# Three row buffers, weights loaded on another condition, Y cleared from SyncE's queue, and redrawn places, in a Mamba layer with routed experts

## What is computed

```python
h = x + mamba(layernorm(x), ...)              # scan: h_t = exp(dt*A) * h_(t-1) + dt*x * B_t, 16 states, 512 channels
m = gelu(layernorm(h) @ mlp_w1.T + mlp_b1) @ mlp_w2.T + mlp_b2
x = layernorm(x + h + m)
scores = softmax(xf @ gate_w.T); _, idx = top_k(scores, 2)       # cw: the weight of each token for each expert
y = einsum("nef,edf->ned", silu(xf @ wg.T) * (xf @ wu.T), wd)    # 8 experts, inner width 128
routed = einsum("ned,ne->nd", y, cw)
shared = silu(xf @ sg.T) * (xf @ su.T) @ sd.T
x = layernorm(x + routed + shared)
```

## Time and profile before

| | us |
|---|---|
| median of three runs | 5452.79 |
| lowest and highest of them | 5439.62 and 5469.59 |
| the profiled execution | 5453.14 |
| its span in the trace | 5451.4 |

### The profile page before, as it was taken

How to read it: one execution, slowest core, us unless ns; L and a number is a source line. 1 busy time by engine, 2 the same in 40 slices (tenths; PEclk the granted TensorE clock), 3 DMA queues, 4 the chain that set the end, 5 groups by cost and what they waited for, 6 DMA issues and landing times. The chain is left out here.

```text
span 5451.4 us, 75865 instructions
## 1 busy us (share of the span) xinstructions
PE 4273.5 (78%) x20928; PEld 2954.8 (54%) x20928; DVE 4418.7 (81%) x6313; ACT 3392.8 (62%) x6338; POOL 3581.1 (66%) x2252
## 2 busy tenths in 40 slices
PE   3777877788888888878887778888878888888873
PEld 2455555455555555555555555555555566555652
DVE  5889988978888887788888788788888888878741
ACT  4666666556666656666666666666667776667633
POOL 4666666656566566666677666677767785677743
PEclk7898898999899999899999899899999999988987
DMA  1122522233333333332332332333334442455555
GB/s 57 61 76 80 136 81 79 81 101 116 107 127 111 107 92 98 89 104 84 88 95 77 97 103 84 87 92 89 94 110 113 125 132 88 141 141 145 155 141 152
DMA packets 357156, 563.53 MB, mean 103 GB/s; under 512 B 40433, under 2 KB 203378, under 8 KB 356610
## 3 DMA queue, kind: packets, MB, share of 16 engines
q1 hardware_dynamic: 253250, 398.07, 24.4%
q0 software_dynamic: 49152, 67.27, 6.1%
q10 hardware_dynamic: 54336, 93.34, 5.1%
HBM read 440.66 MB, written 186.05 MB: 115 GB/s over the span
## 5 line engine op out<-in xcount | busy, mean ns | idle before, releaser
L585 POOL TENSOR_TENSOR dBx<-dtx,Bbc 128x1024 f32<-128x1024 f32 x1024 | 2424.0, 2397 | 749.3 <-DVE hs L1224 721.5
L1224 DVE TENSOR_TENSOR_SCAN hs<-ps,dBx 128x512 f32<-128x512 f32 x2048 | 2397.8, 1208 | 179.7 <-ACT ps L750 132.9
L750 ACT ACTIVATE ps<-dt,A 128x512 f32<-128x512 f32 x2048 | 1389.4, 690 | 598.4 <-DVE hs L1224 538.5
L969 PE MATMUL ps<-ident,hs 128*128 128x128 f32 x8192 | 1325.6, 302 | 366.4 <-DVE acc L1240 186.7
L969 PEld LDWEIGHTS ps<-ident,hs 128*128 128x128 f32 x8192 | 1037.7, 154 | 858.8 <-issue 408.2
L1240 DVE SCALAR_TENSOR_TENSOR acc<-ps,C_tok,acc 128x512 f32<-128x512 f32 x1792 | 1282.0, 740 | 237.1 <-PE ps L969 218.6
L642 POOL DMA_INDIRECT fx<-Y_slots,slots x256 | 403.8, 1577 | 124.8 <-issue 56.7
L618 POOL DMA_INDIRECT X_slots<-xs,slots x256 | 257.1, 1004 | 323.4 <-DVE slots L1356 264.4
L1125 PE MATMUL ps<-xsT,wx 128*128 128x128 f32 x2432 | 339.8, 293 | 99.1 <-ACT xsT L837 99.1
L1125 PEld LDWEIGHTS ps<-xsT,wx 128*128 128x128 f32 x2432 | 317.0, 207 | 130.5 <-issue 127.6
L1213 DVE SCALAR_TENSOR_TENSOR xc<-ps,conv_w,xc 128x511 f32<-128x511 f32 (+2 forms) x384 | 285.5, 744 | 74.3 <-ACT xc L714 65.9
(11 more groups left out here) (210 smaller groups left out, 6090.3 us busy)
## 6 DMA issues: line engine op xcount, KB each, us to landing
Bbc<-B_scratch SPq DMA_DIRECT2D x512, 256.0 KB
wx<-in_experts SPq DMA_DIRECT2D x308, 384.0 KB, 5.3
Y_slots<-zeros ACTq DMA_DIRECT2D x228, 256.0 KB, 3.6
xin<-X_slots SPq DMA_DIRECT2D x308, 128.5 KB, 4.1
Y_slots<-xin SPq DMA_DIRECT2D x308, 128.0 KB
xt<-in_x SPq DMA_DIRECT2D x32, 512.0 KB, 5.6
shared<-xt ACTq DMA_DIRECT2D x32, 512.0 KB
fx<-shared SPq DMA_DIRECT2D x32, 512.0 KB
```

What stands on the lines that cost most here:

```text
L585: pool.tensor_tensor(dBx[u % 3][:], dtx[b % 2][:, 2 * h:2 * h + 2, :], Bbc[g % NBB][:, n % CH:n % CH + 1, :].broadcast_to([P, 2, T]), ALU. ...
L750: act.activation(psA[s % 2][:], dt[b % 2][:, j, :], ACT.Exp, scale=A[:, j, n:n + 1]).then_inc(s_dA, 1)
L969: i = pe.transpose(psH[w % 2][:, j * P:(j + 1) * P], hs[(n * CT + j) % NHB][:, t * P:(t + 1) * P], ident[:])
L1224: dve.tensor_tensor_scan(hs[s % NHB][:], psA[s % 2][:], dBx[s // 2 % 3][:, s % 2, :], 0.0, ALU.mult, ALU.add).then_inc(s_scan, 1)
```

## The change

Four things. The routed rows get three buffers (NR = 3) in place of two, with the semaphores s_xin and s_Y_out by p % 3; the weights keep two. A pair's weights are loaded once the last product of pair p - 2 has ended (s_down_e), its rows once the store of pair p - 3 has landed. The clearing of Y_slots moves from ACT's queue to SP's. All tables in `AT` are new, for every engine. Cut to the core (of the tables two stand for all):

```diff
-    "SP_experts": [110.03, 122.95, 127.33, 133.34, 144.56, 147.72, 148.88, 158.4, 159.99, 163.15, 164.6, 166.33],
+    "SP_clear": [7.35, 11.99, 91.18, 91.18, 92.21, 94.14, 94.38, 94.38, 94.38, 94.38, 94.38, 94.6, 94.6, 94.6, 98.58,
+        98.58, 98.58, 98.58, 98.58],
+    "SP_experts": [108.63, 127.61, 129.07, 131.43, 134.25, 143.48, 153.05, 156.74, 158.83, 162.2, 162.7, 164.76],
...
-    PERIODS, PAIRS_MAX, FINS_MAX = NB + 3, 12, 3
+    PERIODS, PAIRS_MAX, FINS_MAX, NR = NB + 3, 12, 3, 3
...
-        xin = [sb(f"xin{i}", [P, 2, ROW]) for i in range(2)]
+        xin = [sb(f"xin{i}", [P, 2, ROW]) for i in range(NR)]
...
-            return 32 * ((p - k) // 2 + 1)
+            return 32 * ((p - k) // NR + 1)
...
+            def clear():
+
+                for i in range(2):
+                    rows = Y_slots[i].rearrange("(p n a) d -> p n (a d)", p=P, a=2)
+                    for k in range(CLEARS):
+                        yield first[i] + groups[i] * k // CLEARS
+                        if (i, k) == (0, 0):
+                            sp.wait_ge(s_zeros, 16)
+                        sp.dma_start(rows[:, k, :], zeros[:, 0:2 * D]).then_inc(s_Y_cleared[i], 16)
...
-                        g, k = group_of_pair[p], p % 2
+                        g, k = group_of_pair[p], p % NR
...
                         if p >= 2:
-                            sp.wait_ge(s_Y_out[k], stores(p - 2, k))
+                            sp.wait_ge(s_down_e, p - 1)
                         for i in range(2):
                             e = sp.value_load(where[g % 2][0:1, 1, tile + i:tile + i + 1], min_val=0, max_val=NE * P)
+                            sp.dma_start(wx[p % 2][:, i, :], a["experts"].rearrange("e p f -> (e p) f")[
+                                bass.ds(e, P), :]).then_inc(s_wx[p % 2], 16)
+                        if p >= NR:
+                            sp.wait_ge(s_Y_out[k], stores(p - NR, k))
+                        for i in range(2):
                             r = sp.value_load(where[g % 2][0:1, 0, tile + i:tile + i + 1], min_val=0, max_val=ROWS - P)
-                            sp.dma_start(wx[k][:, i, :], a["experts"].rearrange("e p f -> (e p) f")[
-                                bass.ds(e, P), :]).then_inc(s_wx[k], 16)
                             sp.dma_start(xin[k][:, i, :], X_slots[g % 2][bass.ds(r, P), :]).then_inc(s_xin[k], 16)
...
-            def clear():
-
-                for i in range(2):
-                    rows = Y_slots[i].rearrange("(p n a) d -> p n (a d)", p=P, a=2)
-                    for k in range(CLEARS):
-                        yield first[i] + groups[i] * k // CLEARS
-                        if (i, k) == (0, 0):
-                            act.wait_ge(s_zeros, 16)
-                        act.dma_start(rows[:, k, :], zeros[:, 0:2 * D]).then_inc(s_Y_cleared[i], 16)
```

137 lines of the change are left out of this document (68 added, 69 removed), and 29 rows, old and new, of the table AT.

## The result

The changed kernel takes 5311.32 us (median of 4 runs, 5298.0 to 5320.7) where the kernel before takes 5446.2 us (4 runs): a ratio of 0.9748, 95% interval 0.972 to 0.9776. A second measurement, among the experiments, gave 5302.48 us and 0.974 (0.9713 to 0.9766).

A forecast was written before the change was run, and what follows sets the result against it. DVE, busy 81%, plus its gaps was taken to bound the kernel. Terms 44 + 10 + 8 + 18 + 10 + 6 + 8 - 12 = 92 us off 5453 gave 5361 us, range 5320 to 5410.

The forecast's parts named there:

- signs of the profile: Expected after: PE's row waits under 30 us, third-pair tanh wait 3 to 4, five-pair batches near 158 to 160.
- even: At a new group: last Bbc load lands at 3034, POOL wanted it at 3034.11; 1 us charged per group.
- the queue: SP's queue, Bbc loads behind clears and pads: -12 us, 1 for each of seven new groups, 5 for the rest.
- The 28 us of the late batches and the tail: Loads no longer behind stores: 18 us in batches with ten pairs, 10 us in the tail.
- Places drawn anew: Two more acc updates on DVE before the third pair's tanh wait: 8 us gain, bounds -40 and +36.
- the clears: 228 DMAs leave ACT's queue: 0.5 us a batch in the first twelve, 6 us, bounds 0 and 44.
- Those of the third pair count in full: PE's waits for rows in twelve five-pair batches: third pair worth 44 us, second pair 10 us.
- Seven-pair batches: PE's load waits there, one a batch of about 2 us, would go: 8 us gain.
- (A): Loads come early but time doesn't follow, DVE's gap stays; a quarter of the gain kept, 5430 us; chance 0.11.
- (B): ACT's redrawn order stalls the scan, 4 us in each of 32 batches: 5489 us; chance 0.08.
- (C): SP's queue binds, Bbc loads come late and the clears' gain is gone: 5432 us; chance 0.05.
- (D): More gain: five-pair batches at 157.7 us, late batches give 40, redrawing its whole 36: 5288 us; chance 0.10.

The follow-up runs named there:

- e7: Kernel before with the third buffer and the two new waits, all tables and clears as before: 0.9955.
- e11: Kernel before with third buffer, its waits, pairs' loads ahead of stores, and new places of the Bbc loads and B_scratch store: 0.9895.
- e13: Kernel after with the old tables of ACT, DVE, PE and POOL, and the clears back on ACT: 0.9849.
- e5: Kernel after with the old tables of ACT, DVE, PE and POOL; all of SyncE new, clears included: 0.9814.
- e17: Kernel after, unchanged, measured a second time: 5302.48 us, 0.974.
- e2: Kernel before with the new tables of ACT, DVE, PE and POOL; SyncE, buffers and clears as before: 0.9988.
- e3: Kernel after with POOL's four tables of the kernel before: 0.9741.
- e16: Kernel after with POOL's old tables and the two-buffer wait in the four- and five-pair batches: 0.9748.
- e6: Kernel after, but in four- and five-pair batches a pair's rows wait for the store of the pair two back: 0.974.
- e18: Kernel after with PE's and POOL's tables of the kernel before: 0.9747.
- e15: Kernel after with PE's seven tables of the kernel before: 0.9731.
- e9: Kernel after with the third pair's loads in five-pair batches again behind the second pair's store: 0.9783.
- e10: Kernel after with the third pair's loads behind the second pair's store and the second pair's behind the first's: 0.9805.
- e14: Kernel before with only the 228 clears moved to SyncE, and SP_behind with them: 0.9999.

## Why the prediction was right and wrong

**Right: the direction and the signs of the profile.** PE's waits for the rows are under 30 us (3.6), the five-pair batches take 157 us (161 with a new group), the third pair's gate waits 2.58 us where 3 to 4 were named, POOL waits for Bbc in batches 7 to 12, hidden, and doesn't at the new groups behind the twelfth batch, "even" as worked out from the earlier trace rows.

**Wrong: the size, and what it is made of.** 92 forecast, 135 measured, a factor of 1.5 and outside the range. In the chain of kernels from before to after, by ratios times 5446 us, against the terms of the sum:

```
buffers and waits (e7)                      -25
+ order of loads, stores, Bbc (e11)         -33
+ SP's other places (e13)                   -25    sum -82; forecast 90 for all loads, -7 for the queue: 83
+ clears on SP (e5)                         -19    forecast 6, -5 for the queue: 1
+ computing engines (after)                 -36    forecast 8
```

Each step is known to some 15 to 20 us only, and another order of the steps gives other sizes. That the load terms came out within 1 us is luck. By the stages cut above, us saved against the kernel before (each column is one execution, so a few us in a row mean nothing):

```
                        forecast, loads    e13     e5   after   e17
7 batches, no pairs                  0     1.7   19.7    12.6  15.7
12 five-pair                        54    92.8   97.0   101.6 108.0
6 four-pair                          0    -0.4    5.8     8.5  12.4
4 seven-pair                         8     1.8  -13.6   -10.9 -10.6
all behind them                     28     0.6   -3.9    20.6  23.9
```

Too little in the five-pair batches and too much behind them cancel. The 28 us of the late batches and the tail were priced on waits for loads; all of SyncE new (e5) brings none of them, and the 21 us seen in the kernel after come with the computing engines.

**The step that failed most is "Places drawn anew"**: I priced the two acc updates on DVE at 17 us, halved that without a reason in a row, and added it. The runs show 36 us beside the new SyncE and 7 beside the old one (e2). Nor do the 36 lie where I looked for them. The nine five-pair batches that open no group take 1405.1 us in e5 and 1414.9 and 1410.6 in the two profiles of the kernel after, so the gate behind two more acc updates brings nothing there, although DVE's wait for the tanh falls from 239 to 129 us over the whole span. What e5 lacks is found at the new groups (14 to 17 us in three batches) and behind the seven-pair batches (25 to 28). Which row of DVE or ACT does it stays open. **The second is the clears**: I took 0.5 us a batch from DVE's wait for ACT (7.4 us in two batches) "with clears or without about the same share". The first seven batches alone gave some 16 us, over 2 a batch; the bound of 3.7 x 12 was nearer in size than the value taken. That the gain depends on the rest (0, 19 or 7 us) no bound said.

**The third and second pair.** "Those of the third pair count in full", 44 + 10, has the two the wrong way round: taken back out of the kernel after, where DVE's gate stands later in its order, the third costs next to nothing by the stages and the second some 20 us (19 and 12 by the ratios, both within what these tell apart). The table of stages seems to say the opposite, with 102 us gone in the twelve five-pair batches. Both are true, because other parts work in the same batches: the buffers and waits in the old order (e7) take 35 us out of them, the computing engines in the old order (e2) 49, all of SyncE (e5) 97. These do not add up, so no single price of the early loads exists. Had I judged by stages only, I would have put it all down to the loads.

**Seven-pair batches**: forecast -8, measured +11 in the profile. Two things are seen in it. POOL's new places go with it: three kernels without them are shorter there than their neighbours that have them, 644.0 (e3) against 662.9 and 662.7, 650.6 (e16) against 659.5 (e6), 649.1 (e18) against 653.1 (e15), though their whole time isn't. And the clock does: e9 and e10 have the kernel after's order there and take 669 and 673 us, at 0.91 and 0.90 for its 0.92. How much belongs to either is open.

**The rivals.** (A) fell, the time followed; but its ground, that an earlier load need not make the batch shorter, is what e9 shows for the third pair. (B) did not come. (C) did not come in the kernel after, and is what happens with one table less: 0.9748 turns into 1.0121 when the Bbc places are taken back, with 123 of the 189 us in the profile in and behind the seven-pair batches, where (C) had no price. I had charged the Bbc loads' new places only with a risk (-12), and not seen that the old ones could not have carried the early loads at all. (D), 5288 us, was nearer (23 us off, the forecast 50): its five-pair batches at the 157.7 us of the four-pair ones came (157), and the redrawing's "whole 36" in size; its 40 us in the late batches did not.

Open: the order at a new group (44.9 us in three batches, of which e2 alone has 24 and e7 14) was not tried alone; nor was what e13 adds split into the fx load, the last group's loads and the rest.

## What to carry to other kernels

When one in-order queue carries several kinds of loads, moving one kind forward pays only if the others are placed again around its waits: here loads ahead of stores cost 101 us and the places of the other loads alone 36, and together they gained 57. So for every wait that is moved, list what stands behind it in the queue and when its user wants it, in the denser batches first (the seven-pair ones lost 71 us where the five-pair ones gained 32). And a redrawn order on the engines that compute should be priced with the change and without it, for its worth came out as 36 and 7 us. A price read from an engine's wait should be checked by taking that one piece back out, and by the stage in which it should show.

## What the hardware showed

**Stretches with the same orders differ by the clock.** From the thirteenth batch on, e14 has on every engine the order of the kernel before. Batches 17 and 18, before and in e14:

```profile
2660.40:2974.70 314.30, 253.91 (x1262) 174.15 (x1262) 270.59 (x377) 208.13 (x389) 223.44 (x138) 0.95 0.32 88
```

```profile
2638.80:2965.20 326.40, 266.37 (x1261) 180.29 (x1260) 271.04 (x377) 208.24 (x389) 223.48 (x138) 0.90 0.31 85
```

The same rows take 12.1 us more, at a mean granted clock of 0.90 in place of 0.95 (1 is the level of 2.4 GHz, 0.5 that of 1.2; e14 is at 0.50 from 2678.8 to 2688.8 us); PE's busy time rises by 12.5 us, DVE's by 0.5. The way to the time is seen in DVE's waits for PE, before and in e14:

```profile
DVE acc L1240 <- PE ps L969: 11.8, 11, 3.4
```

```profile
DVE acc L1240 <- PE ps L969: 23.0, 14, 3.6
```

Between e14's own runs the clock goes from 0.905 (5471 us) to 0.918 (5420 us). So of the stages above, single differences of a few us a batch are not to be read as the change's.

**Between kernels a higher clock is no faster kernel.** With PE's and POOL's old places (e18) the clock is 0.921 to 0.927 in its runs and the time 5304 us; in the kernel after, run beside it, 0.909 to 0.915 and 5302 us.
